# A router's normed row transposed by the DMA queue in 16-bit halves instead of by the matmul engine

## The chip, the cores and the metric

The kernel runs on one core of a Trainium2 chip. A core has a matmul engine (TensorE, PE in the profile; its weight loads, PEld, overlap), VectorE (DVE), ScalarE (ACT), GpSimd (POOL) and a queue engine (SyncE, SP) that here issues all DMAs. They run side by side and meet at semaphores. The metric is the device time of one execution in microseconds (us): 465.68 for the kernel before, the median of 3 runs (465.28 to 467.05).

## The reference

Four residual stages over x (4 x 512 rows of 512 values), each on a layer norm of x:

```
x = x + tanh(g_xattn[0]) * smooth_quant_expert(ln(x), fside, ctx)      # a
x = x + tanh(g_ffn[0])   * bit_ffn(ln(x))                              # b
x = x + tanh(g_xattn[1]) * (ln(x) @ softmax(q k^T)^T)                  # c
x = x + tanh(g_ffn[1])   * moe(ln(x))                                  # d, e

def bit_linear(x, w, b):        # b: rows rounded to 8 bits, weights to -1, 0, 1
def moe(x):
    logits = x @ router_w.T                    # 8 experts
    gate = softmax(logits) * top2_mask(logits)
    a = silu(x @ down_w.T)                     # 8 experts x 16
    return sum over experts of gate * (a @ up_w.T)
```

## The kernel before

The 2048 rows are 16 tiles of 128 rows (NT = 16). Stage a and all preparation of weights and attention come first; from about 200 us on, the rest is a software pipeline over tiles, written out as one `tile_step(i)` for each engine. Step i works on stage b of tile i, finishes b and does c of tile i-1, does the router's product (d) of tile i-2 and the experts' sum (e) of tile i-3. Nothing is scheduled at run time: each engine runs its own list in order, and semaphores hold an instruction until its inputs are there.

Names in the lists: `b_chunk(i, c)` is one of four chunks of 512 hidden columns, a gate and a value product of 4 matmuls each (L1823), into PSUM banks that ACT has filled with biases (`gate_seed`, `val_seed`, L1423, L1433). ACT's `b_gate` (L1408) is the silu, DVE's `b_product` multiplies and takes a row maximum (L912, L914), `b_quantise` (L917 to L929) and ACT's `b_scaled` (L1414) write the rounded row, four DMA transposes (L442) turn it, and `b_output` (16 matmuls, L1918) multiplies it in the next step. `x_transpose` (L432) turns the rounded input of the next tile's chunks. `c_norm` (L1351 into qT_room), `c_spread` (PE transposes, L1805), `c_transposed` (ACT copy, L1247) and `c_attend` (L1830) are stage c. Stage d is `d_norm` (L1351 too), `d_spread` (4 PE transposes of 128x128 32-bit blocks into a PSUM bank, L1805), `d_transposed` (ACT copy back, L1247), `d_project` (L1852), `d_logits` on DVE, `softmax_power` on POOL (L645) and `d_hidden` on ACT (L1398). Stage e is `d_gate` on DVE, `e_spread`, `e_transposed`, `e_expand` (L1878) and `e_add`. POOL's `q_root`, `c_root` and `d_root` (L614, L615, L620) make the reciprocal deviation and the shift of each norm, and `q_seeds` (L635) the factor of the seeds.

In ACT's and PE's lists of the kernel before a d tile goes like this:

```
ACT: ... b_gate(i,1)  d_norm(i-2)  val_seed(i,2)  gate_seed(i,3)  q_norm(i+1)  e_transposed(i-3)  d_transposed(i-2) ...
PE:  ... b_output(i-1)  d_spread(i-2)  e_spread(i-3)  b_chunk(i,2)  d_project(i-2)  b_chunk(i,3)  c_spread(i-1)  e_expand(i-3)  c_attend(i-1)
```

After step 15 comes a tail for the last tiles, with filler matmuls (`clock_held`) and a last output in halves.

Of the kernel before, what the change touches and what calls it, by code (L numbers as in the profile page):

```python
# [8 lines left out]
F8 = mybir.dt.float8e4  # L9
ALU = mybir.AluOpType  # L10
ACT = mybir.ActivationFunctionType
AX_X = mybir.AxisListType.X

P = 128
# [30 lines left out]
def flamingo_gated_kernel(nc, x, fside, ctx_in, g_xattn, g_ffn, gate_w, gate_b, val_w, val_b, out_w, out_b,  # L45
# [6 lines left out]
    T = S // P  # L52
# [8 lines left out]
    with ExitStack() as ctx:  # L61
# [107 lines left out]
        silu_h, a_d, a_dt = (row_room[:, r * EI:(r + 1) * EI] for r in range(3))  # L169
        ln_b = q_room[:, 0:D]  # L170
# [81 lines left out]
        def project_bank(n):  # L252
            return p_out[:, 1, :] if n < NT - 2 else p_gate[:, 1, :]
# [51 lines left out]
        d_y, d_exp, d_silu, d_a, d_at, d_at_copied, d_up = (sem(f"d_{n}") for n in ("y", "exp", "silu", "a", "at", "at_copied", "up"))  # L305
        stored = sem("stored")
# [44 lines left out]
        with nc.Block() as block:  # L351
            @block.sync
            def _(sp):
# [99 lines left out]

                x_load(0, 0)
                fside_load(0)
                w_load(0, 0)
                w_load(0, 2)
                w_load(0, 3)
                w_load(0, 1)
# [44 lines left out]
                for i in range(NT):  # L504
                    if 2 <= i < NT - 1:
                        x_transpose(i + 1)
                    for c in range(HC if i < NT - 1 else HC // 2):
                        p_transpose(i, c)
                    if i >= 3:
                        store(i - 3)  # L510
                for n in range(NT - 3, NT - 1):
                    store(n)
# [4 lines left out]
            def _(pool):  # L517
# [112 lines left out]

                def q_seeds(n):
# [119 lines left out]
                for i in range(2, NT - 1):  # L751
                    tile_step(i)
                d_root(NT - 3)
                c_root(NT - 2)
                softmax_power(NT - 3)
                d_root(NT - 2)
                c_root(NT - 1)
                softmax_power(NT - 2)
                d_root(NT - 1)

            @block.vector
            def _(dve):
# [141 lines left out]
                def b_product(n, c):  # L904
# [9 lines left out]
                    return nc.vector.tensor_reduce(mu4[:, c:c + 1], cols, AX_X, ALU.max, apply_absolute_value=True)  # L914

                def b_scales(n, link):
# [14 lines left out]
                def b_quantise(n, link):  # L931
                    b_scales(n, link)
# [39 lines left out]
                def d_norm_last():  # L972
                    dve.wait_ge(d_tr, NT - 1)
# [55 lines left out]
                def tile_step(i):  # L1029
                    b_link = Chain(dve, b_chain, (HC + 3) * i)  # L1030
                    if i + 1 < NT:
                        q_statistics(i + 1)
                    c_add(i - 2)
                    d_statistics(i - 2)
                    b_link(b_product(i, 0))
                    if i >= 3:
                        d_gate(i - 3)
                    b_link(b_product(i, 1))
                    b_add(i - 1)
                    c_statistics(i - 1)  # L1040
                    if i + 1 < NT:
                        q_maximum(i + 1)
# [4 lines left out]
                    if i + 1 < NT:  # L1047
                        q_dequant(i + 1)
                    if i >= 3:
                        e_add(i - 3)  # L1050

                link0, link1 = Chain(dve, b_chain, 0), Chain(dve, b_chain, HC + 3)
# [141 lines left out]
                link0(b_product(0, 0))  # L1194
                link0(b_product(0, 1))
# [5 lines left out]
                link0(b_product(0, 2))  # L1201
# [949 lines left out]
```

## Time and profile before

| | |
|---|---|
| time of 3 runs | 465.68 us (465.28 to 467.05) |
| span of the profiled execution | 460.9 us |
| median less the span: what lies around it | 4.8 us |
| PE, DVE, ACT, POOL busy | 416.9, 380.3, 350.2, 221.1 us |
| HBM read, written | 28.33, 4.19 MB |

The span runs from the first to the last instruction. The three times are of other executions than the profiled one, whose own time is not among them; its span is set against them by the 4.8 us. Busy time is the sum over the span; what matters for the change is one step of the pipeline, so the rows below are mostly of a single step.

### The profile page before, as it was taken

To read this page: it belongs to the slowest core of one execution; us is meant where nothing else is said; L and a number is where in the kernel's file an instruction comes from. 1 tells how busy PE (TensorE), PEld (TensorE's weight loads), DVE (VectorE), ACT (ScalarE), POOL (GpSimd) and SP (SyncE) were. 2 spreads that over 40 slices of the span, in tenths; PEclk is the share of its full clock that TensorE was granted. 3 is DMA by queue.
4 is the path that set the end of the run, shared out by engine and by line. 5 is a ranking of instruction groups with operands and counts; after the bars stand their busy time and mean duration, and the time that the engine had idled before them with its cause. 6 is when DMAs were issued, how large, how long until landed. Compare 5 with 4: busy or idle time off the path is not lost.

```text
span 460.9 us, 7370 instructions
## 1 busy us (share of the span) xinstructions
PE 416.9 (90%) x2183; PEld 243.3 (53%) x2183; DVE 380.3 (83%) x955; ACT 350.2 (76%) x574; POOL 221.1 (48%) x343
## 2 busy tenths in 40 slices
PE   7477779888988977799999999999999999999986
PEld 7366556646665434345545545544554554554563
DVE  2898799999978788387889889889889889988853
ACT  1399898877899998578778788788778777777532
POOL 3285967577886745544333424333333333341220
PEclk9978999999999998999999999999999999999999
DMA  7999984691895202321231232132123123122101
GB/s 299 389 320 232 293 285 84 147 280 27 216 207 148 59 12 48 56 46 25 41 73 25 68 70 46 48 70 58 35 69 60 44 62 76 36 59 68 46 26 46
DMA packets 84952, 49.53 MB, mean 107 GB/s; under 512 B 70952, under 2 KB 73512, under 8 KB 83888
## 3 DMA queue, kind: packets, MB, share of 16 engines
q1 hardware_dynamic: 84912, 49.06, 41.4%
q8 instruction: 17, 0.28, 0.3%
q14 instruction: 23, 0.19, 0.1%
HBM read 28.33 MB, written 4.19 MB: 71 GB/s over the span
## 4 chain that ended last, share of the span: by engine, by line
PE 64%; DVE 13%; POOL 6%; issue 5%; ACT 5%; DMA 4%; SPq 2%; POOLq 0%; DVEq 0%; ACTq 0%
PE p_gate L1823 11%; PE p_val L1823 11%; PE p_out L1830 11%; PE p_out L1918 10%; PE p_tr L1805 3%; PE p_out L1852 3%; PE p_out L1878 3%; DVE rowmax L832 3%; DMA att_t<-in_L_ffn_val_w 2%; PE p_gate L1660 2%; SPq L426 1%; DVE h_max L792 1%; ACT val_t L1287 1%; PE p_val L1782 1%; DMA qT_room<-q_room 1%
## 5 line engine op out<-in xcount | busy, mean ns | idle before, releaser
L1823 PE MATMUL p_val<-val_t,q_room 128*128 128x512 fp8e4 x256 | 66.6, 383 | 2.6 <-ACT p_val L1433 2.6
L1823 PE MATMUL p_gate<-gate_t,q_room 128*128 128x512 fp8e4 x256 | 66.6, 383 | 0.2 <-DMA q_room<-q_room 0.2
L1830 PE MATMUL p_out<-att_t,qT_room 128*128 128x512 f32 x120 | 55.4, 603 | 0.7 <-ACT qT_room L1247 0.7
L1918 PE MATMUL p_out<-out_t,ws_f 128*128 128x512 fp8e4 x240 | 54.4, 379 | 1.2 <-DMA ws_f<-ws_f 1.2
L614 POOL TENSOR_TENSOR rstd<-mv,ln_eps 128x1 f32<-128x1 f32 x48 | 9.1, 190 | 89.9 <-DVE mv L883 82.8
L1423 ACT ACTIVATE p_gate<-w_slots,seed_scale 128x512 f32<-128x512 f32 x64 | 43.6, 682 | 9.9 <-POOL seed_scale L635 8.6
L912 DVE TENSOR_TENSOR act_f<-p_val,ctx_sb 128x512 f32<-128x512 f32 x64 | 44.1, 690 | 7.9 <-PE p_val L1823 5.3
L1408 ACT ACTIVATE ctx_sb<-p_gate,bcol 128x512 f32<-128x512 f32 x64 | 43.5, 682 | 9.3 <-PE p_gate L1823 4.3
L914 DVE TENSOR_REDUCE mu<-act_f 128x1 f32<-128x512 f32 x64 | 43.9, 686 | 2.2
L1433 ACT ACTIVATE p_val<-w_in,seed_scale 128x512 f32<-128x512 f32 x64 | 43.3, 680 | 0.0
L1823 PEld LDWEIGHTS p_val<-val_t,q_room 128*128 128x128 f16 x256 | 25.2, 99 | 33.7 <-ACT p_val L1433 3.1
L641 POOL TENSOR_TENSOR x_all<-x_all,q_room 128x512 f32<-128x512 f32 x16 | 20.3, 1269 | 45.1 <-ACT q_room L1351 40.0
L1823 PEld LDWEIGHTS p_gate<-gate_t,q_room 128*128 128x128 f16 x256 | 25.2, 99 | 29.4 <-issue 9.1
L1918 PEld LDWEIGHTS p_out<-out_t,ws_f 128*128 128x128 f16 x240 | 23.3, 98 | 29.9 <-DMA ws_f<-ws_f 2.4
L1830 PEld LDWEIGHTS p_out<-att_t,qT_room 128*128 128x128 f32 x120 | 21.5, 189 | 30.8 <-issue 21.1
L645 POOL TENSOR_TENSOR ey<-e_base,y 128x8 f32<-128x8 f32 x15 | 24.8, 1654 | 23.5 <-DVE y L1005 23.5
L881 DVE BATCH_NORM_STATS2 stats<-x_all 128x6 f32<-128x512 f32 x46 | 31.6, 687 | 1.5 <-POOL shift L620 0.2
L615 POOL TENSOR_TENSOR rstd<-rstd,half_neg 128x1 f32<-128x1 f32 x48 | 26.4, 551 | 3.8
L1247 ACT ACTIVATE qT_room<-p_tr 128x512 f32<-128x512 f32 x32 | 19.0, 595 | 11.7 <-PE p_tr L1805 11.7
L1351 ACT ACTIVATE qT_room<-x_all,shift,rstd 128x512 f32<-128x512 f32 x30 | 24.1, 802 | 4.8 <-POOL shift L620 4.8
L1247 ACT ACTIVATE row_room<-p_tr 128x128 f32<-128x128 f32 (+1 forms) x20 | 6.8, 338 | 24.0 <-PE p_tr L1870 24.0
L938 DVE SCALAR_TENSOR_TENSOR x_all<-p_out,tanh_g,x_all 128x512 f32<-128x512 f32 x30 | 22.0, 734 | 2.4 <-PE p_out L1878 1.3
(247 smaller groups left out, 980.2 us busy)
## 6 DMA issues: line engine op xcount, KB each, us to landing
att_t<-in_L_ffn_out_w SPq DMA_DIRECT2D x6, 1024.0 KB, 6.5
x_all<-in_x SPq DMA_DIRECT2D x4, 1024.0 KB, 6.1
att_t<-in_L_ffn_gate_w SPq DMA_DIRECT2D x4, 1024.0 KB, 13.5
out_dram<-x_all SPq DMA_DIRECT2D x15, 256.0 KB, 2.3
w_in<-in_fside_BxS2xS SPq DMA_DIRECT2D x3, 1024.0 KB, 7.7
att_t<-in_L_ffn_val_w SPq DMA_DIRECT2D x3, 1024.0 KB, 8.3
ctx_sb<-in_ctx SPq DMA_DIRECT2D x4, 512.0 KB, 7.8
side<-in_L_ffn_val_w SPq DMA_DIRECT2D x1, 1024.0 KB, 14.4
```

Source lines behind the costliest of these rows:

```text
L615: root = nc.gpsimd.tensor_tensor(rstd[:, s:s + 1], rstd[:, s:s + 1], half_neg[:, 0:1], ALU.pow)
L645: nc.gpsimd.tensor_tensor(ey[:, :], e_base[:, :], y[:, :], ALU.pow).then_inc(d_exp, 1)
L881: link(nc.vector.bn_stats(stats[:, s, :], tile_of(n)))
L912: nc.vector.tensor_tensor(cols, p_val[:, c % 2, :], silu_g[:, c % 2, :], ALU.mult).then_inc(u_done, 1)
L914: return nc.vector.tensor_reduce(mu4[:, c:c + 1], cols, AX_X, ALU.max, apply_absolute_value=True)
L1247: nc.scalar.activation(dst, src, ACT.Copy).then_inc(done, 1)
L1408: nc.scalar.activation(silu_g[:, c % 2, :], p_gate[:, c % 2, :], ACT.Silu, scale=col(CG)).then_inc(silu_done, 1)
L1423: nc.scalar.activation(p_gate[:, c % 2, :], bias_gate[:, c * 512:(c + 1) * 512], ACT.Copy, scale=seed_scale[:, n % 2, 0:1]).then_inc(gate_ ...
L1433: nc.scalar.activation(p_val[:, c % 2, :], bias_val[:, c * 512:(c + 1) * 512], ACT.Copy, scale=seed_scale[:, n % 2, 1:2]).then_inc(val_see ...
L1823: last = nc.tensor.matmul(bank[:, c % 2, :], x_t[n % 2][:, k * P:(k + 1) * P], w_t[m][:, k, cols], start=False, stop=k == KD - 1, skip_gro ...
L1830: last = nc.tensor.matmul(p_out[:, 0, :], lt_c[:, k * P:(k + 1) * P], att_t[:, bass.ds((n // T) * (KD * S) + k * S, S)], start=k == 0, sto ...
L1918: last = nc.tensor.matmul(p_out[:, 0, :], p_t[:, k * P:(k + 1) * P], w_t[2][:, k, :], start=k == 0, stop=k == KH - 1)
```

## The change

The transposes of ln_d (`d_spread`, PE) and their copy out of PSUM (`d_transposed`, ACT) go for tiles 0 to 13. In their place POOL splits the 32-bit row into two planes of 16-bit halves (`d_split_planes`), SP issues one DMA transpose over both planes (1024 columns of 16 bits, `d_transpose`), and ACT joins the halves to 32-bit values (`d_merged`). Tiles 14 and 15 keep the old way.

The lists are written in another order too. PE's `d_project` moves from between chunks 2 and 3 to behind `c_spread`, into bank 0 of p_tr, and `e_expand` to behind chunk 2. On ACT `q_scaled` goes behind `c_transposed`, `d_hidden` behind two seeds. On DVE `d_logits` goes behind the fourth product and `e_add` ahead of it. On POOL `q_seeds` goes ahead of `q_bias`, and `softmax_power` comes last. SP issues the four transposes of p16 as 0, 2, 1, 3. Steps 2, 3, 14, 15 are written out with the same pattern. `w_load` gets an argument it doesn't use, and DVE's `Chain` objects are only made elsewhere.

```diff
+        d_planes, d_planes_t = (side[:, r * D:(r + 1) * D] for r in range(2))
         def project_bank(n):
-            return p_out[:, 1, :] if n < NT - 2 else p_gate[:, 1, :]
+            return p_tr[:, 0, :] if n < NT - 2 else p_gate[:, 1, :]
...
+                def d_transpose(n):                                   # SP
+                    sp.wait_ge(d_split, n + 1)
+                    need(sp, d_lt, n)
+                    sp.dma_start_transpose(out=d_planes_t.bitcast(U16).rearrange("p (k r) -> p k r", r=P),
+                                           in_=d_planes.bitcast(U16)).then_inc(d_planes_landed, 16)
+                def tile_step(i):
+                    x_transpose(i + 1)
+                    p_transpose(i, 0)
+                    p_transpose(i, 2)
+                    p_transpose(i, 1)
+                    p_transpose(i, 3)
+                    store(i - 3)
+                    d_transpose(i - 1)
...
+                def d_split_planes(n):                                # POOL
+                    pool.wait_ge(d_ln, n + 1)
+                    need(pool, d_planes_landed, 16 * n)
+                    nc.gpsimd.tensor_copy(d_planes.bitcast(U16).rearrange("p (h c) -> p h c", h=2),
+                                          ln_d.bitcast(U16).rearrange("p (c h) -> p h c", h=2)).then_inc(d_split, 1)
                 def tile_step(i):
                     q_root(i + 1)
                     d_root(i - 2)
+                    d_split_planes(i - 2)
+                    c_root(i - 1)
+                    q_seeds(i + 1)
                     q_bias(i + 1)
-                    c_root(i - 1)
                     softmax_power(i - 2)
-                    q_seeds(i + 1)
...
                 def tile_step(i):                                     # DVE
...
-                    b_link(b_product(i, 2))
-                    d_logits(i - 2)
-                    b_link(b_product(i, 3))
-                    b_quantise(i, b_link)
-                    if i + 1 < NT:
-                        q_dequant(i + 1)
-                    if i >= 3:
-                        e_add(i - 3)
+                    b_product(i, 2)
+                    e_add(i - 3)
+                    b_product(i, 3)
+                    d_logits(i - 2)
+                    b_quantise(i)
+                    q_dequant(i + 1)
...
+                def d_merged(n):                                      # ACT
+                    act.wait_ge(d_planes_landed, 16 * (n + 1))
+                    need(act, d_mm, n)
+                    nc.scalar.activation(lt_d.bitcast(U16).rearrange("p (c h) -> p h c", h=2),
+                                         d_planes_t.bitcast(U16).rearrange("p (h c) -> p h c", h=2), ACT.Copy).then_inc(d_lt, 1)
...
                 def e_expand(n):                                      # PE
                     pe.wait_ge(d_at_copied, n + 1)
-                    pe.wait_ge(d_y, projected)
-                    pe.wait_ge(d_silu, projected)
+                    need(pe, d_x, n)
```

PE, one step from `b_output` (16 matmuls from ws_f) to `c_attend` (from att_t); ln_d and ln_c both lie in qT_room, so both transposes read alike. The list before:

```order
L1918 MATMUL p_out<-out_t,ws_f 128x512 x16
L1805 MATMUL p_tr<-ident,qT_room 128x128 x4
L1870 MATMUL p_tr<-ident,row_room 128x128
L1823 MATMUL p_gate<-gate_t,q_room 128x512 x4
L1823 MATMUL p_val<-val_t,q_room 128x512 x4
L1852 MATMUL p_out<-router_down_t,qT_room 128x136 x4
L1823 MATMUL p_gate<-gate_t,q_room 128x512 x4
L1823 MATMUL p_val<-val_t,q_room 128x512 x4
L1805 MATMUL p_tr<-ident,qT_room 128x128 x4
L1878 MATMUL p_out<-up_t,row_room 128x512
L1830 MATMUL p_out<-att_t,qT_room 128x512 x4
```

The same stretch of PE's list in the changed kernel:

```order
L2127 MATMUL p_out<-out_t,ws_f 128x512 x16
L2080 MATMUL p_tr<-ident,row_room 128x128
L2034 MATMUL p_gate<-gate_t,q_room 128x512 x4
L2034 MATMUL p_val<-val_t,q_room 128x512 x4
L2087 MATMUL p_out<-up_t,row_room 128x512
L2034 MATMUL p_gate<-gate_t,q_room 128x512 x4
L2034 MATMUL p_val<-val_t,q_room 128x512 x4
L2013 MATMUL p_tr<-ident,qT_room 128x128 x4
L2062 MATMUL p_tr<-router_down_t,qT_room 128x136 x4
L2041 MATMUL p_out<-att_t,qT_room 128x512 x4
```

The first transpose of the two is gone, `e_expand` stands where `d_project` stood, and `d_project` stands between `c_spread` and `c_attend`.

ACT, from `q_norm` (into q_room) through stage c's copy, before; the second L1247 is `d_transposed`, the third `c_transposed`, L1373 is `q_scaled` and L1398 `d_hidden`:

```order
L1351 ACTIVATE q_room<-x_all,shift,rstd 128x512
L1247 ACTIVATE row_room<-p_tr 128x128
L1247 ACTIVATE qT_room<-p_tr 128x512
L1433 ACTIVATE p_val<-w_in,seed_scale 128x512
L1408 ACTIVATE ctx_sb<-p_gate,bcol 128x512
L1373 ACTIVATE q_room<-q_room,bcol 128x512
L1351 ACTIVATE qT_room<-x_all,shift,rstd 128x512
L1408 ACTIVATE ctx_sb<-p_gate,bcol 128x512
L1398 ACTIVATE row_room<-p_out 128x128
L1247 ACTIVATE qT_room<-p_tr 128x512
```

And now; L1506 is `d_merged`, L1498 `q_scaled`, L1531 `d_hidden`:

```order
L1476 ACTIVATE q_room<-x_all,shift,rstd 128x512
L1566 ACTIVATE p_val<-w_in,seed_scale 128x512
L1372 ACTIVATE row_room<-p_tr 128x128
L1556 ACTIVATE p_gate<-w_slots,seed_scale 128x512
L1541 ACTIVATE ctx_sb<-p_gate,bcol 128x512
L1566 ACTIVATE p_val<-w_in,seed_scale 128x512
L1506 ACTIVATE qT_room<-side 128x2x512
L1476 ACTIVATE qT_room<-x_all,shift,rstd 128x512
L1541 ACTIVATE ctx_sb<-p_gate,bcol 128x512
L1372 ACTIVATE qT_room<-p_tr 128x512
L1498 ACTIVATE q_room<-q_room,bcol 128x512
L1556 ACTIVATE p_gate<-w_slots,seed_scale 128x512 x2
```

The join stands directly ahead of `c_norm`, and `q_scaled` behind `c_transposed` instead of ahead of `c_norm`.

## Rows read from the trace of the kernel before

**Rows 1.** The page: busy time by engine, and the granted clock in 40 slices.

```profile
PE 416.9 (90%) x2183; PEld 243.3 (53%) x2183; DVE 380.3 (83%) x955; ACT 350.2 (76%) x574; POOL 221.1 (48%) x343
PEclk9978999999999998999999999999999999999999
```

**Rows 2.** Busy time of PE, PEld, DVE, ACT, POOL, clock: step 11, step 2.

```profile
351.46:368.12 16.66, 16.66 (x77) 8.42 (x76) 14.78 (x45) 13.19 (x23) 6.23 (x12) 1.00 0.31 57
201.66:218.21 16.55, 15.86 (x74) 8.09 (x73) 13.10 (x38) 13.28 (x21) 7.44 (x14) 1.00 0.22 43
```

**Rows 3.** Timeline of PE, step 2, steps 10 and 11: start, duration, instruction.

```profile
214.67 3.70 PE L1830 MATMUL p_out<-att_t,qT_room 128*128 128x512 f32 x8 [0.69 <-ACT qT_room L1247]
...
341.71 0.60 PE L1805 MATMUL p_tr<-ident,qT_room 128*128 128x128 f32 x4
342.15 0.27 PE L1870 MATMUL p_tr<-ident,row_room 128*128 128x128 f32 x1
342.25 1.03 PE L1823 MATMUL p_gate<-gate_t,q_room 128*128 128x512 fp8e4 x4
...
343.98 1.09 PE L1852 MATMUL p_out<-router_down_t,qT_room 128*128 128x136 f32 x8
344.91 1.03 PE L1823 MATMUL p_gate<-gate_t,q_room 128*128 128x512 fp8e4 x4
...
347.07 1.04 PE L1878 MATMUL p_out<-up_t,row_room 128*128 128x512 f32 x2
347.95 3.68 PE L1830 MATMUL p_out<-att_t,qT_room 128*128 128x512 f32 x8
351.46 1.03 PE L1823 MATMUL p_gate<-gate_t,q_room 128*128 128x512 fp8e4 x4
...
354.91 3.62 PE L1918 MATMUL p_out<-out_t,ws_f 128*128 128x512 fp8e4 x16
```

**Rows 4.** Timeline of ACT, then of POOL, step 11: seed, gate, c_norm; d's and c's shift.

```profile
359.76 0.70 ACT L1433 ACTIVATE p_val<-w_in,seed_scale 128x512 f32<-128x512 f32 x1
360.37 0.69 ACT L1408 ACTIVATE ctx_sb<-p_gate,bcol 128x512 f32<-128x512 f32 x1
...
361.99 0.80 ACT L1351 ACTIVATE qT_room<-x_all,shift,rstd 128x512 f32<-128x512 f32 x1
...
354.37 0.26 POOL L620 TENSOR_SCALAR shift<-mv,rstd 128x1 f32<-128x1 f32 x1
...
361.36 0.27 POOL L620 TENSOR_SCALAR shift<-mv,rstd 128x1 f32<-128x1 f32 x1
```

**Rows 5.** Groups by form on ACT and POOL, whole span: busy us, mean ns.

```profile
L1247 ACT ACTIVATE qT_room<-p_tr 128x512 f32<-128x512 f32 x32 | 19.0, 595 | 11.7 <-PE p_tr L1805 11.7
L1287 ACT ACTIVATE gate_t<-p_val,less_round 128x1024 fp8e4<-128x1024 f16 x8 | 8.4, 1105 | 0.4 <-PE p_val L1682 0.4
L1247 ACT ACTIVATE up_t<-p_val 128x512 f32<-128x512 f32 x1 | 1.1, 1114 | 0.5 <-PE p_val L1654 0.5
L546 POOL TENSOR_SCALAR o_hs<-att_t,inv_gamma_w 128x1024 f16<-128x1024 f32 x4 | 4.5, 1117 | 3.6 <-DVE inv_gamma_w L776 3.4
```

**Rows 6.** SP's timeline; landing of L432's transposes; DMA share and GB/s (last columns).

```profile
333.03 5.13 SPq L442 DMA_TRANSPOSE ws_f<-ws_f  x4
345.45 1.19 SPq L432 DMA_TRANSPOSE q_room<-q_room  x1
349.69 6.35 SPq L442 DMA_TRANSPOSE ws_f<-ws_f  x4
...
DMA to landing us min/median/max: 2.4/2.4/2.4
...
346.65:347.25 0.60, 0.60 (x6) 0.60 (x5) 0.41 (x1) 0.22 (x2) 0.60 (x1) 1.00 1.01 202
```

**Rows 7.** The chain that ended last, in order of time: in and behind the last step.

```profile
433.34 0.66 DVE x_all L938
439.67 0.66 PE p_tr L1805 x4
```

More of the change, by code:

```diff
@@ L9 @@
 F8 = mybir.dt.float8e4
+U16 = mybir.dt.uint16
 ALU = mybir.AluOpType
@@ L1221, in _ @@
                 o_dequantise(3, 2)
[L1222 to L1223 removed]
+                b_product(1, 3)
+                b_quantise(1)
                 q_dequant(2)
                 o_dequantise(3, 3)
[L1226 to L1230 removed]
+                q_statistics(3)
+                c_add(0)
+                d_statistics(0)
@@ new lines, in _ @@
+                b_product(2, 0)
+                b_product(2, 1)
+                b_add(1)
+                c_statistics(1)
+                q_maximum(3)
+                b_product(2, 2)
+                b_product(2, 3)
+                d_logits(0)
+                b_quantise(2)
+                q_dequant(3)
+                q_statistics(4)
+                c_add(1)
+                d_statistics(1)
+                b_product(3, 0)
+                d_gate(0)
+                b_product(3, 1)
+                b_add(2)
@@ new lines, in _ @@
+                c_statistics(2)
+                q_maximum(4)
+                b_product(3, 2)
+                e_add(0)
+                b_product(3, 3)
+                d_logits(1)
+                b_quantise(3)
+                q_dequant(4)
+                for i in range(4, NT - 2):
+                    tile_step(i)
+                q_statistics(15)
+                c_add(12)
+                d_statistics(12)
+                b_product(14, 0)
+                d_gate(11)
+                b_product(14, 1)
@@ new lines, in _ @@
+                b_add(13)
+                c_statistics(13)
+                q_maximum(15)
+                b_product(14, 2)
+                e_add(11)
+                b_product(14, 3)
+                d_logits(12)
+                b_quantise(14)
+                q_dequant(15)
+                c_add(13)
+                d_statistics(13)
+                b_product(15, 0)
+                d_gate(12)
+                b_product(15, 1)
+                b_add(14)
+                c_statistics(14)
+                b_product(15, 2)
@@ L1617, in _ @@
                 gate_seed(2, 1)
-                for i in range(2, NT):
-                    tile_step(i)
+                b_gate(2, 0)
+                gate_seed(2, 2)
+                d_norm(0)
+                b_gate(2, 1)
+                q_norm(3)
+                val_seed(2, 2)
+                gate_seed(2, 3)
+                b_gate(2, 2)
+                val_seed(2, 3)
+                d_merged(0)
+                c_norm(1)
+                b_gate(2, 3)
+                c_transposed(1)
@@ new lines, in _ @@
+                val_seed(3, 3)
+                d_merged(1)
+                c_norm(2)
+                b_gate(3, 3)
+                c_transposed(2)
+                q_scaled(4)
+                gate_seed(4, 0)
+                gate_seed(4, 1)
+                d_hidden(1)
+                val_seed(4, 0)
+                b_scaled(3, 2)
+                b_scaled(3, 3)
+                val_seed(4, 1)
+                for i in range(4, NT - 2):
+                    tile_step(i)
+                b_gate(14, 0)
@@ new lines, in _ @@
+                gate_seed(14, 2)
+                d_norm(12)
+                b_gate(14, 1)
+                q_norm(15)
+                val_seed(14, 2)
+                e_transposed(11)
+                gate_seed(14, 3)
+                b_gate(14, 2)
+                val_seed(14, 3)
+                d_merged(12)
+                c_norm(13)
+                b_gate(14, 3)
+                c_transposed(13)
+                q_scaled(15)
+                gate_seed(15, 0)
+                gate_seed(15, 1)
```

342 lines of the change are left out of this document (229 added, 113 removed).

## Prediction, written before the result was known

> **What bounds the kernel now.** I read the page first: PE is busy 90% of the span, DVE 83%, ACT 76%, and PE's clock is granted in full after the first quarter [rows 1]. An average over stages doesn't say what a step costs, so the busy time of one step of the pipeline comes next. Step 11 lasts 16.66 us, PE is busy for all of it at clock 1.00, DVE for 14.78, ACT for 13.19, POOL for 6.23 [rows 2]. PE's timeline shows no idle time in it: each group starts where the one ahead has issued its last matmul. In such a row the duration runs to the modelled end; what PE gives up is the distance to the next start. So d_spread costs 342.15 - 341.71 = 0.44 us, e_spread 0.10, d_project 0.93, e_expand 0.88, c_attend 3.51, a chunk (gate and value half) 1.73, and b_output 3.46 [rows 3]. In steps 2 to 15 the timeline shows one hole on PE, 0.69 us in step 2, where c_attend waits for ACT's copy of ln_c because no e_expand stands between [rows 3]; PE is busy 15.86 of 16.55 us there [rows 2]. The pipeline is bound by PE's own work, and of the others DVE is the next.
>
> **What goes.** Four transposes in each of 14 steps, 0.44 us each, on the path: the instruction behind them starts earlier by all of it. ACT's copy of 0.595 us goes too [rows 5]; ACT has 3.5 us of room in a step, so that is no gain in itself. Step length becomes 16.66 - 0.44 = 16.22 us if nothing is late.
>
> **What comes, and whether it is late.** All times here count from a step's first matmul (351.46 for step 11).
>
> PE's new list: b_output ends at 6.92, e_spread 7.03, chunk 2 8.76, e_expand 9.64, chunk 3 11.37, c_spread 11.81, d_project 12.73, c_attend 16.22. PE wants ln_c at 11.37, the joined ln_d at 11.81.
>
> Stage d's chain: its shift is made at 354.63, or 3.17 [rows 4]. d_norm takes 0.80, to 4.0. The split is new: no row shows a 16-bit copy on POOL. Its nearest row is the 1024-element operation of 1.12 us [rows 5]; the floor is nothing gained over half of that, 0.56, the ceiling twice it, 2.2. I take 1.12: end 5.15. POOL waits in this stretch for c's statistics in any case, whose shift is made at 361.63, or 10.17 [rows 4], so c_root, the seeds and softmax_power behind the split are not pushed.
>
> The DMA transpose is new in its size, 1024 columns. One of 512 columns keeps SP 1.19 us, its packets start when the issue ends (they fill the engines from 346.65 to 347.25 for an issue at 345.45), and it lands 2.4 after the issue: 1.2 issue, 0.7 packets, 0.5 to the semaphore [rows 6]. With twice the columns, issue and packets doubled one after the other give 2.4 + 1.3 + 0.5 = 4.2; if only the packets double 3.1; if everything doubles 4.9. I take 4.2, the plain reading of the row. SP is free for it: the four transposes of p16 are out 5.13 us after they start [rows 6], in the new order by about 3.9, and a store of 0.6 follows; the issue is at 5.2. The planes land at 9.4.
>
> ACT's join: no row joins 16-bit halves. The nearest is 1024 elements in 1.11 us [rows 5]; the floor is the 0.595 of the copy that it replaces; the ceiling is twice 1.11, 2.2, since one 512-element copy with a scattered output took 1.114 where the plain one takes 0.595 [rows 5]. I take 1.1. ACT itself is ready at 9.3: chunk 2's gate half is there at 7.03 + 1.03 = 8.06, then follow b_gate and a seed at 0.61 from start to start [rows 4]. So the join runs 9.4 to 10.5 and c_norm to 11.3, against the 11.37 at which PE wants it. c_norm could not have begun before 10.2 anyway. It fits, with 0.1 us to spare by this reading, 0.2 more in what ACT itself leaves and 0.6 if the landing is 3.65.
>
> The copy of up_t is where the Trainium skill speaks: its page "SBUF — State Buffer" (section "Door 1: The DMA port swizzle") says that an access stays at full rate only if at least two neighbours fall in a 16-byte line. up_t's output goes in steps of 16 bytes, and the trace agrees, 1.114 us. The join writes in steps of 4 bytes, so by that rule it runs at the plain rate, 1.1 us. If the step as such were what slows it, it would be the 2.2 of my ceiling. The same stands for the split, whose reads have steps of 4 bytes: the page "GPSIMD Engine Reference" (section "Performance pitfalls for Q7 kernels") sees a slower read only above 8 bytes. No run here shows either yet.
>
> **What moves.** d_project in place of e_expand between c_spread and c_attend covers ACT's copy of ln_c as well (0.93 for 0.88). d_logits now ends after the fourth product, and by adding up DVE's rows b_quantise comes about 0.4 us nearer to the end of the step than before. Its four transposes are first needed 3.46 us into the next step, in pieces 0.87 apart, and the last is issued about 2.6 into it and lands at 5.1, wanted at 6.1. q_scaled moves a good 2.5 us later, behind c_transposed: it ends at 13.2, the x_transpose lands 2.4 later at 15.7, and PE wants it at 16.22. That cushion was over 3 us and is now 0.5. The seeds come sooner, since softmax_power no longer stands ahead of q_seeds. DVE has 1.4 us of room left in a step. No cost while these hold.
>
> **The sum.** Steps 3 to 14: 12 x 0.44 = 5.2. Step 2 has nothing to run in the place of e_expand, and now d_project covers the hole of 0.69; but there PE wants ln_c 1.0 earlier and can't have it before about 11, so of 0.44 + 0.69 I count 0.5. Step 15 and the tail: PE gains 0.44 again, but the last row is quantised where it was (d_logits comes ahead of it, e_add's 0.66 [rows 7] has moved into a wait), and two PE transposes wait for it, so that is lost; the same e_add then lets d_gate, c_add and the norm of tile 14 come about 0.4 earlier, which is what ends last there (d_spread at 439.67 [rows 7]). I count 0.4. Together 6.1 us. From that 0.6 goes for late transfers: a group of four transposes took 6.35 us once instead of 5.13 [rows 6], and the two cushions of 0.1 to 0.5 us would pass much of such a delay on to PE. Forecast: span 460.9 - 5.5 = 455.4, and with the 4.8 us around it 460.2 against 465.68.
>
> **Rivals.**
>
> 1. The d chain is late by more than its cushion, through the landing: 4.9 instead of 4.2. The planes arrive at 10.1, c_norm ends at 12.0, PE waits 0.6 in each of some 12 steps: 7.2 us, and 460.2 becomes 467.4. For it: no row shows that size. Against it: packets and semaphore of the short one are seen apart, and only the first two should grow.
>
> 2. The other side: the join costs 2.2 us. It starts at 9.4, ends at 11.6, c_norm ends at 12.4 and PE waits 1.0 us in 12 to 13 steps, 12.5 us in all: 460.2 + 12.5 = 472.7, slower. It decides from a join of about 1.2 us on, and turns the change into a loss from about 1.6. With a landing of 3.65 it would be 470. For it: up_t's row. Against it: the step is 4 bytes, not 16. A split of 2.2 gives the same kind of loss, about 1.0 a step.
>
> 3. DVE becomes the bound. It is busy 14.78 us by the busy time, but its chained small instructions leave gaps, and its own waits on PE in a step come to only about 1 us. If half of the gain runs into that: 465.68 - 2.8 = 462.9.
>
> 4. The x_transpose with its 0.5 us cushion is regularly late, or transfers disturb each other now that SP issues 2.4 us more in a step (1.2 + 5.1 + 0.6 before): PE waits 0.2 to 0.3 in a step, 462 to 464.
>
> 5. The change doesn't do what it says: the transposes were hidden. The rows speak against it: PE has no idle time behind them. It would give 465.7.
>
> **How the numbers follow.** What a measurement of this kernel can tell from no change is about 0.5%, 2.3 us, so faster is below 463.35 and slower above 468.0. Forecast 0.62 (its own range 458.6 to 462.2); rival 1 0.09, in the band of no change for the most part; rival 2 with the late split 0.10, slower; rival 3 0.06, mostly faster; rival 4 0.11, two thirds faster; rival 5 0.02. That makes faster 0.75, same 0.14, slower 0.11. The range is 458.4 to 467.5: it takes in rivals 1, 3 and 4, and leaves out rival 2 and a little below.
>
> **What would show it.** Right: 4 instead of 8 PE transposes out of qT_room in a step, and steps of 16.2 us with no idle time on PE. The split 1.1 us, the wide transpose 2.4 us on SP and about 4.2 to landing, the join 1.1. Wrong: ACT idle before the join for more than a few tenths, PE waiting at c_spread for ACT's c_norm, or at the first chunk for the x transpose; a join near 2 us; a step length that stays above 16.5.

## The result, and the profile after

The changed kernel takes 469.51 us (median of 6 runs, 466.66 to 471.13), the kernel before 465.87 in the same batch (6 runs): a ratio of 1.0080, 95% interval 1.0052 to 1.0107. It is slower by 0.8%; forecast was 1.2% faster. The profiled execution took 469.37 us, its span is 467.5 instead of 460.9. Here 1.9 us lie around the span, and 1.8 in the kernel before of a later batch (465.03 us, span 463.2). So the traced execution of the kernel before took about 462.7 us, 3 less than its median. The 4.8 us that its table sets around the span are 1.8 around it and 3 of a fast execution, and the 6.6 us between the two spans overstate the 3.6 between the medians.

A step that nothing disturbs does what was forecast. PE's timeline of the changed kernel, from one `b_output` (L2127) to the next:

```profile
377.27 3.62 PE L2127 MATMUL p_out<-out_t,ws_f 128*128 128x512 fp8e4 x16
...
385.15 0.65 PE L2013 MATMUL p_tr<-ident,qT_room 128*128 128x128 f32 x4
385.63 1.09 PE L2062 MATMUL p_tr<-router_down_t,qT_room 128*128 128x136 f32 x8
386.56 3.62 PE L2041 MATMUL p_out<-att_t,qT_room 128*128 128x512 f32 x8
...
393.47 0.81 PE L2127 MATMUL p_out<-out_t,ws_f 128*128 128x512 fp8e4 x3
```

That is 16.20 us without idle time where it was 16.66 [rows 3]. The new operations, from the answers on their lines (least, median and longest ns, or us to landing):

```profile
L680 POOL COPY side<-qT_room x14: 1036/1036/1037, 208.3 to 426.8; 128x1024 uint16<-128x1024 uint16 x14
...
L450 SPq DMA_TRANSPOSE side<-side x14: 1232/1239/1302, 209.3 to 428.5; - x14
...
DMA to landing us min/median/max: 3.0/3.1/3.5
...
L1506 ACT ACTIVATE qT_room<-side x14: 1333/1339/1346, 212.8 to 433.4; 128x1024 uint16<-128x1024 uint16 x14
```

Split 1.04, landing 3.1, join 1.34. ACT never sits idle for a landing. In the step of the PE rows above, the join and the c_norm behind it stand in ACT's timeline like this:

```profile
383.10 1.34 ACT L1506 ACTIVATE qT_room<-side 128x1024 uint16<-128x1024 uint16 x1
384.30 0.79 ACT L1476 ACTIVATE qT_room<-x_all,shift,rstd 128x512 f32<-128x512 f32 x1
```

The join holds ACT for 1.20 us (383.10 to 384.30), and c_norm ends at 385.09, 0.06 ahead of the 385.15 at which PE takes it. But PE is busy 413.7 us (88% of the span, 90% before [rows 1]), and it waits where it did not. Its waits from 207 us on (total us, times, longest):

```profile
PE p_out L2127 <- DMA ws_f<-ws_f: 5.0, 5, 1.4
PE p_gate L2034 <- DMA q_room<-q_room: 3.1, 3, 1.3
PE p_val L2116 <- DMA ws_f<-ws_f: 1.1, 1, 1.1
PE p_tr L2013 <- ACT qT_room L1476: 0.7, 1, 0.7
```

The first is `b_output` waiting for a piece of p16, the second the first chunk waiting for `x_transpose`, the third the last output. The fourth is c_norm in step 2, where the kernel before waited as long for c's copy [rows 3]. A hole below is a place where PE stands idle for a transfer. These are all the holes of the first two kinds, in PE's timeline (the idle time in brackets counts from the modelled end of the row ahead, so each costs about 0.16 more):

```profile
220.75 1.04 PE L2034 MATMUL p_gate<-gate_t,q_room 128*128 128x512 fp8e4 x4 [0.88 <-DMA q_room<-q_room]
241.76 2.76 PE L2127 MATMUL p_out<-out_t,ws_f 128*128 128x512 fp8e4 x12 [0.31 <-DMA ws_f<-ws_f]
255.08 1.04 PE L2034 MATMUL p_gate<-gate_t,q_room 128*128 128x512 fp8e4 x4 [1.26 <-DMA q_room<-q_room]
294.37 1.04 PE L2127 MATMUL p_out<-out_t,ws_f 128*128 128x512 fp8e4 x4 [0.63 <-DMA ws_f<-ws_f]
310.40 2.76 PE L2127 MATMUL p_out<-out_t,ws_f 128*128 128x512 fp8e4 x12 [1.38 <-DMA ws_f<-ws_f]
344.51 2.76 PE L2127 MATMUL p_out<-out_t,ws_f 128*128 128x512 fp8e4 x12 [1.35 <-DMA ws_f<-ws_f]
373.81 1.04 PE L2034 MATMUL p_gate<-gate_t,q_room 128*128 128x512 fp8e4 x4 [0.98 <-DMA q_room<-q_room]
428.42 2.77 PE L2127 MATMUL p_out<-out_t,ws_f 128*128 128x512 fp8e4 x12 [1.31 <-DMA ws_f<-ws_f]
```

**What stands behind a hole.** Two x_transposes of the changed kernel, from the DMA view: the late one whose wait ends at 255.08 (249.6 to 253.2 us), then an undisturbed one (386.9 to 391.2). Columns: packets, MB, share; then the median us to landing.

```profile
q1 hardware_dynamic: 542, 0.13, 18.5%
q8 instruction: 1, 0.02, 1.9%
...
q_room<-q_room SPq DMA_TRANSPOSE x1, 4.3
```

```profile
q1 hardware_dynamic: 1088, 0.26, 31.0%
...
ws_f<-ws_f SPq DMA_TRANSPOSE x2, 2.5
q_room<-q_room SPq DMA_TRANSPOSE x1, 2.4
```

The first stretch has a packet of instruction code, at 252.7, 2.0 us behind the issue; the second has none. In the changed kernel's page q8 fetches 17 of 16 KB, q14 23 of 8 KB; the numbers are the same before. In all 18 traces of this study together, 1164 transposes of 512 columns are issued between 215 and 430 us. 748 have no fetch near them (from 1.3 us ahead of their issue to their landing), and every one lands within 2.56 us. 209 land later than 2.8 us, up to 4.84, and all 209 have a fetch there. The other 207 have one too and land within 2.8, so it matters where in the transfer the fetch falls. A 16 KB fetch alone that starts 1 to 2 us behind the issue makes it 3.6 to 4.4, an 8 KB one mostly 3.1 to 3.4.

The Trainium skill says in "Runtime: NRT & Kernel Launch", section "Instruction fetch mechanics", that each engine fetches its code by its own DMA queue in blocks of 16 KiB, 256 instructions. For q8 this trace agrees (16 KB, and a step has 142 instructions on TensorE, one fetch in 1.8 steps); q14's are of 8 KB. The page has the fetch hidden by the slow issue. The fetching engine indeed doesn't stop here: the step with the fetch at 279.2 lasts 16.24 us. What is held up is another transfer.

The kernel before has hardly fewer late landings (10 of 64; after 14 of 65, 11 of 65 in a second trace), but no hole for a transfer. What changed is the cushion, from issue, undisturbed landing and the time PE wants it. x_transpose had 351.46 - 345.45 - 2.4 = 3.6 us; now it is issued at 387.06 and wanted at 390.02: 0.56. The p16 pieces were issued from 333.03 on, 1.28 apart, landing 2.5 later, for 338.26 and on in steps of 0.87: 2.7, 2.3, 1.9, 1.5 us. The new list sends them as 0, 2, 1, 3, and later:

```profile
387.06 1.19 SPq L435 DMA_TRANSPOSE q_room<-q_room  x1
388.95 5.12 SPq L445 DMA_TRANSPOSE ws_f<-ws_f  x4
```

Piece 1 goes out third, at 391.5, lands at 394.0 and is wanted at 394.3. Its cushion is 0.3; pieces 0, 2, 3 have 2.0, 2.5, 0.8.

### The profile page after: what moved, and what is told of

Same layout as the page of the kernel before. It is cut to its first block, busy times and chain, and to the rows that moved or that the text cites. A ratio compares the mean times of both kernels' runs of the same rounds, so it can differ in the third digit from the quotient of the medians.

```text
span 467.5 us, 7339 instructions
## 1 busy us (share of the span) xinstructions
PE 413.7 (88%) x2127; PEld 236.8 (51%) x2127; DVE 388.1 (83%) x955; ACT 357.4 (76%) x574; POOL 234.9 (50%) x357
## 4 chain that ended last, share of the span: by engine, by line
PE 55%; DMA 16%; ACT 9%; DVE 7%; issue 5%; SPq 5%; POOL 3%; ACTq 0%; DVEq 0%; POOLq 0%
PE p_out L2127 10%; PE p_gate L2034 8%; PE p_val L2034 8%; PE p_out L2041 8%; DMA ws_f<-ws_f 6%; DMA q_room<-q_room 3%; PE p_out L2087 3%; SPq L445 3%; DMA att_t<-in_L_ffn_gate_w 2%; DMA att_t<-in_L_ffn_val_w 2%; SPq L429 2%; PE p_tr L2062 2%; PE p_tr L2013 2%; DMA w_in<-in_fside_BxS2xS 2%; PE p_gate L1960 2%
## 5 line engine op out<-in xcount | busy, mean ns | idle before, releaser
L2127 PE MATMUL p_out<-out_t,ws_f 128*128 128x512 fp8e4 x240 | 55.3, 379 | 6.3 <-DMA ws_f<-ws_f 6.3
L1541 ACT ACTIVATE ctx_sb<-p_gate,bcol 128x512 f32<-128x512 f32 x64 | 43.3, 678 | 11.6 <-issue 7.5
L2034 PEld LDWEIGHTS p_gate<-gate_t,q_room 128*128 128x128 f16 x256 | 24.8, 98 | 41.4 <-issue 11.2
L2127 PEld LDWEIGHTS p_out<-out_t,ws_f 128*128 128x128 f16 x240 | 23.0, 98 | 36.2 <-DMA ws_f<-ws_f 9.8
L1476 ACT ACTIVATE qT_room<-x_all,shift,rstd 128x512 f32<-128x512 f32 x30 | 24.1, 805 | 11.8 <-POOL shift L666 11.8
L867 DVE TENSOR_REDUCE h_max<-p_tr 128x1 f32<-128x512 f32 x32 | 20.7, 679 | 4.3 <-PE p_tr L1916 4.1
L654 POOL TENSOR_TENSOR x_all<-x_all,o_hs 128x512 f32<-128x512 f32 x16 | 20.2, 1272 | 6.3 <-DVE o_hs L920 6.1
```

Of the source, the lines that this page charges most:

```text
L1476: nc.scalar.activation(dst, tile_of(n), ACT.Identity, bias=shift[:, s:s + 1], scale=rstd[:, s:s + 1]).then_inc(done, 1)
L1541: nc.scalar.activation(silu_g[:, c % 2, :], p_gate[:, c % 2, :], ACT.Silu, scale=col(CG)).then_inc(silu_done, 1)
L2034: last = nc.tensor.matmul(bank[:, c % 2, :], x_t[n % 2][:, k * P:(k + 1) * P], w_t[m][:, k, cols], start=False, stop=k == KD - 1, skip_gro ...
L2127: last = nc.tensor.matmul(p_out[:, 0, :], p_t[:, k * P:(k + 1) * P], w_t[2][:, k, :], start=k == 0, stop=k == KH - 1)
```

## The experiments

Theory A is the above: late landings, as before, on thin cushions. "Loop" below is the time from `b_output` of step 2 to that of step 15; the kernel before has 216.4 us, the changed one 219.0, each in its trace. Two traces of one kernel differ by up to 1.4 us in it (e14, e15 and e16 repeat the changed kernel, e5 and e9), so smaller differences of the loop say nothing. The ratio is the recorded one to the kernel before in the same batch; it need not be the quotient of two medians.

| run | median us | ratio, 95% | loop us |
|---|---|---|---|
| changed kernel | 469.51 | 1.0080 (1.0052 to 1.0107) | 219.0 |
| e1_order0123 | 466.56 | 1.0046 (1.0020 to 1.0072) | 216.9 |
| e2_qscaled_early | 468.51 | 1.0099 (1.0061 to 1.0136) | 218.7 |
| e3_both | 466.48 | 1.0047 (1.0023 to 1.0071) | 217.4 |
| e4_no_planes | 471.01 | 1.0136 (1.0106 to 1.0166) | 220.4 |
| e5_quantise_first | 468.97 | 1.0047 (1.0014 to 1.0080) | 218.2 |
| e6_before_order0213 | 466.67 | 1.0010 (0.9978 to 1.0042) | 217.9 |
| e7_after_more_code | 471.47 | 1.0109 (1.0068 to 1.0151) | 219.3 |
| e8_before_more_code | 466.25 | 1.0016 (0.9989 to 1.0042) | 216.4 |
| e9_after_shift28 | 467.06 | 1.0031 (1.0004 to 1.0057) | 217.1 |
| e10_order0123_shift28 | 465.78 | 1.0015 (0.9994 to 1.0037) | 217.2 |
| e11_before_shift28 | 466.18 | 1.0027 (1.0000 to 1.0055) | 216.4 |
| e12_after_shift14 | 469.04 | 1.0096 (1.0062 to 1.0130) | 219.7 |
| e13_quantise_first_shift28 | 467.29 | 1.0033 (1.0004 to 1.0063) | 216.1 |
| e14_after_again | 472.65 (one run) | none | 219.0 |
| e15_quantise_first_again | 469.51 (one run) | none | 216.8 |
| e16_shift28_again | 466.17 (one run) | none | 215.7 |

**Cushions wider, or planes out (e1 to e4).**

```diff
e1, SP, steps 2 to 14:
-                    p_transpose(i, 2)
                     p_transpose(i, 1)
+                    p_transpose(i, 2)
e2, ACT:
+                    q_scaled(i + 1)
                     c_transposed(i - 1)
-                    q_scaled(i + 1)
e4, the changed lists with the old transposes:
-                    d_split_planes(i - 2)      (POOL)
-                    d_transpose(i - 1)         (SP)
+                    d_spread(i - 2)            (PE, behind b_output)
```

> The changed kernel with one edit: SP issues the four transposes of p16 as 0, 1, 2, 3 again instead of 0, 2, 1, 3. Theory A (thin cushions: in the order 0, 2, 1, 3 piece 1 goes out third and is wanted second, about 0.5 us after it lands, so that each transfer made 1 to 2 us late by a code fetch stops PE): the waits of b_output on ws_f, 5.0 us in five places in the profiled run of the changed kernel, go to under 1 us, the waits of the first chunk on q_room (3.1 us in three places) stay; 469.5 becomes 464 to 465.5. Theory B (the wide transposes and SP's longer list crowd the DMA queue as such): the same packets are moved in the same time, so the waits stay near 8 us and the time within 1 us of 469.5.

> The changed kernel with one edit: ACT's q_scaled directly ahead of c_transposed instead of behind it, which gives the x transpose about 0.7 us more cushion. Theory A: the waits of the first chunk on q_room go from 3.1 us to about 1.5 in sum (late transfers are late by 1 to 2 us, the cushion becomes about 1.2), those on ws_f stay at about 5; 469.5 becomes 467 to 468.5. Theory B: no change, within 1 us of 469.5.

> Both edits of the two kernels before this one. Theory A: the gains add up, waits on DMA at about 2 us, 462 to 464, faster than the kernel before (465.9). Theory B: within 1 us of 469.5.

> The changed kernel's lists with the planes taken out: PE transposes ln_d again (d_spread behind b_output), ACT copies it out of PSUM at the place of the join, no split, no wide DMA. Theory A: a step is 0.44 us longer (16.66 us), each thin cushion 0.44 us wider, and waits of 3 to 6 us on DMA remain although no wide transpose is left: 469 to 472, about as slow as the changed kernel or slower. Theory B: with the wide transposes gone the waits go, and the time is that of the kernel before or less, 464.5 to 466.

Waits of PE in 207:430, of e1, e2, e3 and e4, in this order:

```profile
PE p_gate L2034 <- DMA q_room<-q_room: 2.1, 2, 1.2
PE p_out L2127 <- DMA ws_f<-ws_f: 2.0, 4, 0.7
PE p_tr L2013 <- ACT qT_room L1476: 1.7, 3, 0.7
```

```profile
PE p_tr L2013 <- ACT qT_room L1476: 1.8, 3, 0.7
PE p_out L2127 <- DMA ws_f<-ws_f: 1.4, 3, 0.8
```

```profile
PE p_tr L2013 <- ACT qT_room L1476: 1.3, 2, 0.7
PE p_out L2127 <- DMA ws_f<-ws_f: 0.9, 2, 0.5
```

```profile
PE p_gate L2022 <- DMA q_room<-q_room: 3.0, 3, 1.2
PE p_out L2115 <- DMA ws_f<-ws_f: 1.2, 2, 0.9
```

e1: with the pieces in order the longest wait on one falls from 1.4 to 0.7 us, and the loop loses 2.1 us; x_transpose's waits stay. Both theories missed the numbers: the waits on ws_f are 2.0 us and not under 1, and the median, 466.56, lies between the 464 to 465.5 of A and the 468.5 to 470.5 of B. The intervals of e1 and of the changed kernel overlap, so e1's gain rests on the loop and the waits and not on the times. e2: with `q_scaled` early no x_transpose is waited for any more, and the waits on ws_f fall too, yet nothing is won, because `c_transposed` comes 0.3 later in every step; the median of 468.5 fits both theories. In e3 an undisturbed step is 16.54 us, and `c_attend` starts 1.17 behind `d_project` where it was 0.93 (386.56 - 385.63):

```profile
256.44 3.62 PE L2127 MATMUL p_out<-out_t,ws_f 128*128 128x512 fp8e4 x16
...
264.81 1.09 PE L2062 MATMUL p_tr<-router_down_t,qT_room 128*128 128x136 f32 x8
265.98 3.70 PE L2041 MATMUL p_out<-att_t,qT_room 128*128 128x512 f32 x8
...
272.98 3.62 PE L2127 MATMUL p_out<-out_t,ws_f 128*128 128x512 fp8e4 x16
```

So both edits together miss the 462 to 464 that I expected: the cushion of x_transpose was bought with the path of stage c. e4 decides between A and crowding by the wide transposes (theory B): without planes it is 471.0, as A says, not 464.5 to 466, and PE waits for the same two kinds of transfer. Its undisturbed steps are 16.59; the planes bring 0.37 us a step and the new lists 0.07.

**The order alone, and a still wider cushion (e5, e6).** e5 is e1 with `b_quantise` ahead of `d_logits` on DVE and `b_scaled` ahead of `d_hidden` on ACT; e6 is the kernel before with the pieces as 0, 2, 1, 3.

> e1_order0123 (planes, transposes of p16 in order 0,1,2,3) and in it DVE runs b_quantise ahead of d_logits and ACT b_scaled(2),(3) ahead of d_hidden. All of the computation is kept. Theory A (DMA transposes that land 1 to 2 us late now and then, on cushions that the new lists made thin): each of the four pieces is issued about 0.45 us sooner after PE's b_output, steps stay 16.2 us, PE's waits on ws_f in 200:430 fall from 2.0 us to under 0.8, those on q_room (x_transpose, cushion unchanged) stay at 1 to 3 us; 464 to 465.5 us beside 466.6 for e1. Theory B (the steps of the planes themselves, or what they add to SP and the DMA engines, cost the time): no change from e1, 466.6.

> The kernel before, with one edit: in steps 2 to 14 SP issues the p16 transposes in order 0,2,1,3. All of the computation is kept. Theory A: in the old lists the pieces come 0.4 us sooner than in the new ones and piece 1, now third, keeps about 1.1 us of cushion, so only the latest landings (over 3.5 us) reach PE: 0 to +1 us beside the kernel before, PE's waits on ws_f in 200:430 at most 1 us more. Rival C (the order alone made the loss, whatever else moved): +2 to +3 us, as much as e1 took back.

```profile
PE p_gate L2034 <- DMA q_room<-q_room: 4.1, 3, 1.8
PE p_tr L2013 <- ACT qT_room L1476: 2.3, 3, 0.8
```

These are e5's waits in 207:430: none on ws_f, as expected. The waits on x_transpose, 4.1, are above the 1 to 3 expected. The others are PE waiting for c_norm (L1476), as in e1 and e2: beyond the 0.7 of step 2, the wide transpose landed twice at 4.8 us, each time with a q8 fetch 2.7 to 2.8 us behind its issue, and its cushion is thin as well. The median, 469.0, is above what either theory gave, and hardly better than the changed kernel's. e6: waits on ws_f of 0.9 us, 2 times, 0.56 for the longest against 1.38 in the changed kernel; the loop is 1.4 us longer, the ratio can't be told from 1. Its two long steps, 17.39 and 17.18 us in place of 16.66, are those of the two waits, so the order alone can make holes, as A says. That they cost e6 time is not shown, and the 2 to 3 us of rival C (the order alone made the loss) did not come.

**Are fetches the cause, or bystanders? (e7 to e12)** First more code that does nothing, on the two idle engines:

```diff
+                    for _ in range(80):
+                        sp.wait_ge(xt_ready, 16)
+                    for _ in range(50):
+                        pool.wait_ge(q_ln, 1)
```

> The changed kernel with 80 waits that are long satisfied on SP behind d_transpose and 50 on POOL behind d_split_planes in each of the steps 4 to 13, where both engines are idle: 1300 instructions more that do nothing, so that the chip has to fetch about a fifth more code. All of the computation is kept. Theory A (an instruction fetch among the packets is what makes a transpose land late): 25 to 32 fetches instead of 21 in the stretch 215:430, more landings over 2.8 us than 14, PE's waits on DMA up by 1.5 to 3 us, time up by as much: 471 to 472.5 us. Rival D (fetches are bystanders; landings are late for another reason, which shows at the same times): same as the changed kernel, 469.5, with as many late landings as it.

> The kernel before with the same 1300 instructions that do nothing (SP behind the store, POOL ahead of q_bias, steps 4 to 13). All of the computation is kept. Theory A: as many more late landings as in e7_after_more_code, but the wide cushions of the old lists (3.6 us on x_transpose, over 2 on the pieces) take most of them: +0 to +1 us beside the kernel before, clearly less than e7 adds to the changed kernel. Rival E (the added instructions cost by themselves, by delaying SP, POOL or PE's own fetches): both kernels slow down by the same 1.5 to 3 us.

This was not decisive, though both medians came out about as A had them. The 1300 waits made 650 instructions, q14's fetches rose from 23 to 29 (e8: 27), q8's stayed at 17, late landings did not rise (12 and 11), and e7's waits on DMA were 5.8 us and not more than the changed kernel's 8.1. That fits with q14 carrying the code of SP and POOL in small pieces and q8 TensorE's, but it doesn't separate A from D (late landings have nothing to do with fetches).

So I moved the q8 fetches instead of adding to them. A few instructions more on TensorE early in the program, and later fetches meet another place of their step:

```diff
+                for _ in range(56):
+                    pe.wait_ge(consts_made, 12)
                 w_total(0)
```

> The changed kernel with 28 more instructions on TensorE (56 waits long satisfied) ahead of w_total(0), in a place near 20 us where PE waits for 4.6 us anyway. Nothing else changes, all of the computation is kept. A 16 KB fetch of TensorE's code comes every 256 of its instructions and a step has 142, so each of these fetches meets its step 28 instructions sooner. Theory A (a 16 KB fetch that starts 0.2 to 2.1 us behind the issue of a transpose makes it land up to 2 us late): all fetches from the eighth on start 2 to 4 us earlier in the pipeline, and the holes move with them: those for x_transpose near 220.8, 255.1 and 373.8 us go, one for x_transpose appears near 340, the ones for ws_f stand in other steps (near 277, 310, 397 and 428); about 5 holes in place of 7, 466.5 to 469 us. Rival D (landings are late for a reason that has nothing to do with fetches): the same holes at the same instructions, 469.5 us.

> e1_order0123 (planes, p16 pieces in order 0,1,2,3) with the same 28 instructions on TensorE ahead of w_total(0). All of the computation is kept. Theory A: again the fetches of TensorE's code start 2 to 4 us earlier and the holes stand at other transposes; steps without one stay at 16.2 us; 464.5 to 467.5 us beside 466.6 for e1. Rival D: the same holes as e1 at the same instructions.

> The kernel before with the same 28 instructions on TensorE ahead of w_total(0). All of the computation is kept. Theory A: as many late landings as before, at other transposes, and none or one reaches PE, since the old lists leave 3.6 us to x_transpose and over 2 us to the pieces: within 1 us of the kernel before. Rival E (the added instructions or the shift cost by themselves): 1 us and more slower, as in e9.

> The changed kernel with 14 more instructions on TensorE (28 waits) ahead of w_total(0). All of the computation is kept. Theory A: the fetches of TensorE's code start 1.5 to 3 us earlier in the pipeline; the holes for x_transpose near 220.8, 255.1 and 373.8 us go, one appears near 337 to 340; fetches that were harmless near 278 and 397 now fall behind the issue of the wide transpose, which then lands at 4 us or more and leaves PE waiting for ACT (c_norm) there; 466.5 to 469.5 us. Rival D: the holes stay where they are, 469.5 us.

In e9 the fetch that stood at 252.7 starts at 244.0, and the x_transpose of that step (issued at 249.94) lands in 2.4 us; the hole of 1.26 at 255.08 is gone, and the one at 373.81 too. The fetch of 339.6 starts at 335.6 and now meets an x_transpose. From the DMA view of e9 in 333.5:337 and from PE's timeline:

```profile
q8 instruction: 1, 0.02, 1.9%
...
q_room<-q_room SPq DMA_TRANSPOSE x1, 4.1
```

```profile
337.82 1.04 PE L2034 MATMUL p_gate<-gate_t,q_room 128*128 128x512 fp8e4 x4 [1.04 <-DMA q_room<-q_room]
```

The same transpose of the changed kernel landed in 2.4, and its step had the ws_f hole of 1.35 instead. That speaks against rival D: 28 instructions that do nothing, 180 us earlier, move holes to where the fetches went, and e16 has the one at 337.7 again, which neither trace of the changed kernel has. The loop lost 1.9 us by it, 3.3 in e16. The list of holes that I expected was not right in all. Counted from the start of the loop the eight fetches in it moved by 0 to 9 us, not by 2 to 4; the first did not move, and the hole behind it (220.0) stayed, while those expected near 277 and 397 didn't come. e12, shifted by half of that, kept the three x_transpose holes that were to go. It got the one near 338 and the wait for c_norm near 400 that were expected: 4 waits of 4.5 us for x_transpose, and no gain. e10 is the best with planes, 465.78, no different from the kernel before. e11: the old lists show nothing of it (loop 216.4, no wait on a DMA in it), though a fetch there met the last output's transposes for 2.0 us, outside the loop.

**Combined, and repeated (e13 to e16).** e13 is e5 with the 28 instructions; e14, e15 and e16 are the changed kernel, e5 and e9 again, for a second trace.

> e5_quantise_first (planes, p16 pieces in order 0,1,2,3, b_quantise ahead of d_logits, b_scaled ahead of d_hidden) with the 28 instructions of e9 on TensorE ahead of w_total(0). All of the computation is kept. Theory A: e5 had no wait left on the p16 pieces and three long ones on x_transpose, each behind a fetch of TensorE's code; with the fetches moved, two of the three x_transposes are no longer met (as in e9), the holes for ws_f stay away, and what remains is one or two x_transposes and now and then the wide transpose: 463 to 465 us, 4 to 5 us below the median of e5 and at or below the kernel before. Rival F (e5's median of 469.0 came from its lists, not from where the fetches fall, since its profiled execution was 3 us faster than its median): no change from e5, 468 to 470 us.

> The changed kernel once more, for a second trace. Theory A (fetches of TensorE's code come at fixed places of its program): the same q8 fetches in the same places of the pipeline and the same five or six long holes (x_transpose near 220.8, 255.1, 373.8; ws_f near 310.4, 344.5, 428.4 in the first trace), shifted with the start of the pipeline by at most 2 us; span 465 to 469. Rival G (where they fall is chance): other holes, another number of them.

> e5_quantise_first once more, for a trace of an execution nearer to its median of 469.0 (its first trace was of 465.9). Theory A: the three x_transpose holes stand where they were; what differs is the start of the pipeline (204.9 in the first, up to 210 in the others of this family) or one or two fetches that now fall behind the issue of the wide transpose. Rival G: holes in other places, more of them, as the 8 KB fetches of the other engines' code drift.

> e9_after_shift28 once more. Theory A: the same holes as in e9 (x near 220.0 and 337.8; ws_f near 292.4, 308.3 and 425.3) and none of those that only the changed kernel has (255.1, 373.8 for x_transpose, 344.5 for ws_f); span 462 to 467. Rival G: other holes.

e13 has a short loop, 216.1, but 467.3 as median, above what A gave (463 to 465) and below rival F (468 to 470: e5's lists are slow as such). Three x_transposes are still waited for, 2.5 us, where one or two were expected. It didn't beat the kernel before, nor did any other. e14 took 472.65 us, span 470.8, and has its holes at the same instructions but one, 3 us later in time. PE's timeline of e14:

```profile
258.05 1.04 PE L2034 MATMUL p_gate<-gate_t,q_room 128*128 128x512 fp8e4 x4 [1.03 <-DMA q_room<-q_room]
297.37 1.04 PE L2127 MATMUL p_out<-out_t,ws_f 128*128 128x512 fp8e4 x4 [0.64 <-DMA ws_f<-ws_f]
313.23 2.76 PE L2127 MATMUL p_out<-out_t,ws_f 128*128 128x512 fp8e4 x12 [1.20 <-DMA ws_f<-ws_f]
347.52 0.82 PE L2127 MATMUL p_out<-out_t,ws_f 128*128 128x512 fp8e4 x3 [1.54 <-DMA ws_f<-ws_f]
```

Only the hole of 373.8 is gone, and there is one of 0.67 us for c_norm two steps on. The loop is 219.0 again; what differs is its start, 210.19 instead of 207.06. e15 (469.51 us) starts at 208.17, e5's first trace at 204.88; of e5's three x_transpose holes the one at 252.8 is gone, which I had expected to stay. e16 (466.17 us) has 292.5, 308.3, 337.7 and 425.2 again and not 220.0.

The three holes that went tell the same story. Counted from the start of the loop, the q8 fetch behind the transpose came at 161.6 us in place of 164.6 in e14, at 42.5 in place of 45.7 in e15, and at 8.7 in place of 11.6 in e16: each about 3 us sooner, and the transpose landed in time. So most holes belong to the program and some to the execution. In the three pairs the start differs by 3.1, 3.3 and 1.5 us, the loop by 0, 1.4 and 1.4.

## Why the prediction was wrong

**Right.** PE's own work bounds a step, and the step became 16.2 us. The transposes were on the path. The d chain held: the split 1.04 for 1.12, the join 1.34 for 1.1. The join as such is above the point of 1.2 from which rival 2 was to decide, but it holds ACT for 1.20, and ACT was ready for it when forecast (9.29 us into the step, for 9.3). The wide transpose keeps SP 1.24 us and not the 2.4 taken, and lands in 3.1 and not 4.2. That is the case worked out beside the one chosen, in which only the packets double; the planes are there about 1 us before ACT wants them. So rivals 1 and 2 stayed away, and c_norm's cushion was the 0.1 forecast. One row was read too kindly, without effect: the clock is not granted in full after the first quarter everywhere, a slice near 180 us has an 8 [rows 1]; in the loop it is 1.00.

**The step that failed** is "From that 0.6 goes for late transfers". I had the row [rows 6]: a group that took 6.35 us in place of 5.13. I read it as a group 1.2 us late once, and not as landings of up to 4.3 us that come in seven of the kernel's 13 steps. In the loop the changed kernel's 13 steps sum to 219.02 us; 13 undisturbed ones would be 210.9. Of the difference, 8.1, 7.9 stands in the six steps with a hole: 16.22 became 17.16, 18.11, 17.01, 17.76, 17.73 and 17.40. Against an expected gain of 5.7 without late transfers, the loop is 2.6 longer. With the 1.5 and 1.1 us in the tail, the term of 0.6 measured 10.5 in this trace. e1, e9 and e4 show the term's cause: the waits on the pieces go down with their order restored, holes move with the fetches, and both kinds stay when the planes go.

**The cushions.** Of the pieces of p16 only the last was worked out ("lands at 5.1, wanted at 6.1"; measured cushion 0.8). Piece 1, which the new order puts third while PE wants it second, has 0.3 and was not looked at. x_transpose's 0.5 was right (0.56), and rival 4 named it. Its price of 0.2 to 0.3 us a step even came true as an average, 3.6 us over 13 steps, though it is nothing in most steps and over 1 us in three; the reason given with it, 2.4 us more on SP in a step, was wrong (1.24). What no rival had is the other 4.3 us, the pieces of p16. Rival 4 had a chance of 0.11, and by itself ended below the kernel before.

**Outside the loop.** The tail (from step 15's `b_output` on) went from 39.4 to 41.4 us instead of down by 0.4: 1.5 of it is the hole at 428.42; the 1.1 us on the last output's pieces is new too. The start came 1.95 later in the trace, with the lists there as they were. Over the traces of all kernels with the changed lists it lies between 204.9 and 212.6, of those with the old ones between 205.1 and 207.6. Two of the four traces of the old lists, e6 (207.6) and e11 (207.3), start as late as the changed kernel's. In the late ones (e14, e2, e7) the granted clock was 0.97 in 50:100, where it was 1.00 in the other fifteen. So a start 1.95 later is within what executions differ by; that the change moves it is neither shown nor excluded.

**Open.** Why a fetch delays a transpose (its packet on the same DMA engine would do it) was not isolated. Fetches could be moved, not taken away, and why some come 3 us sooner in a second execution is open. The planes were not tried on the old lists, with the old cushions; whether they gain there is the test that is missing. Why e5 and e13 have medians 2 to 3 us above their first traces is explained for one execution of e5, by the start of its loop, not for the rest.

## What to carry to other kernels

A transfer's cushion has to be compared with its latest landing, not its usual one. Look for the longest landing in the trace, and when an order of issue changes, work out the cushion of every piece in the order in which it is wanted. In this unrolled program most code fetches came at the same places in each execution. Before judging an edit of less than 1%, look whether the new waits stand beside instruction packets, shift the program by a few instructions, and trace it twice, to see how much of the difference is that.

## What the runs showed of the hardware

An SBUF to SBUF transpose of 16-bit data keeps SP 1.19 us for 512 columns and 1.24 for 1024, and lands in 2.4 to 2.5 and 3.1 us: twice the size costs 0.6. With a 16 KB code fetch 1 to 2 us behind its issue it lands in 3.6 to 4.4, the wide one with the fetch 2.5 to 2.8 behind in 4.7 to 4.8. A copy on POOL that reads 16-bit halves at steps of 4 bytes takes 1.04 us for 1024 elements, where the nearest row, another operation of that size, took 1.12 [rows 5]; on ACT the write at steps of 4 bytes takes 1.34, against 1.11 for the nearest row, of other types [rows 5]. Two waits on a semaphore in a row came out as one instruction (1300 waits, 650 instructions more).
